# Graph propagation and a state-space block on one core: single accumulators in round two, separate banks for the block's outputs, per-row scalars computed once, row shifts on ScalarE

## The chip, the cores and the metric

The kernel runs on one core of one Trainium2 chip. The engines that matter are TensorE (PE: matmuls; PEld: its weight loads), VectorE (DVE), ScalarE (ACT), GpSimd (POOL) and the DMA queue of SyncE (SP). Each has its own queue of instructions, worked off in order; semaphores couple them. The metric is the device time of one launch in microseconds (us), lower is better.

## The reference, cut to what matters

Two layers, each added to its input. The first is two rounds of attention over a graph with 4096 nodes and 128 features; the second is a Mamba2 block (4 heads of 64, 64 states, chunks of 128 rows) over the same 4096 rows.

```python
# layer 1, on xn = layernorm(x); a, temp, h0 given; adj is 4096 x 4096 of 0 and 1
e = leaky_relu(xn @ a[:F] + (xn @ a[F:]).T, 0.2)
U = softmax(where(adj > 0, e, -9e15), axis=1)
rowsum = sum(U * 0.5 * U, axis=1)
feat = f1(U @ xn, xn, rowsum, temp)           # round one, then a soft threshold
out = f2(U @ feat, feat, rowsum, h0, temp)    # round two: a second product with U
x = x + out
# layer 2, on layernorm(x), in 32 chunks of 128 rows
z, xBC, dt = split(ln(x) @ W_in)
xh, B, C = split(silu(causal_conv4(xBC)))
Y = (C B^T * decay) (xh dt) + C h_prev * exp(cum) + xh * D   # h_prev: state carried over chunks
out = rmsnorm(Y * silu(z)) @ W_out @ W_lin + b_lin
```

The softmax is never formed. With leaky_relu the weight of an edge is one of two products, each a factor of the row times a factor of the column, so `U @ Y` is two masked matrix products: accumulator A for edges with a positive logit, accumulator C for the others. Each accumulator is scaled by a factor of its row (`roww[.., 0]`, `roww[.., 1]`) and the two are added. Y is stored as a high and a low fp32r half, so one product has 256 columns.

## The kernel before, in words

N = 4096 rows are 32 tiles of 128 (`NT`). **Start** (to about 82 us of the profile): layer norm of x, column factors `colw`, row factors `roww` (from `hcol`, made by `row_shift` on VectorE, lines 723 to 729), the products Y (`y_product` on GpSimd, `y_high` on ScalarE, line 1014, `y_low_a` on VectorE, line 626), and the first edge codes (`codes`, line 642: 128x512 codes of 1 byte from the transposed adjacency). **Round one** (to about 401 us): 8 groups of 4 tiles; adjacency comes in by DMA, ScalarE takes signs, TensorE transposes, VectorE makes codes, ScalarE and VectorE unpack them into masks A and C, and TensorE multiplies. The codes of all tiles are spilled to DRAM.

**Round two** (from about 409 us) is a software pipeline written out by hand: `schedule` calls `slot(s_, ...)` for 37 slots on every engine, 12 of them through a hardware loop body of 4 slots repeated, the others unrolled. Slot s holds the second product with U for tile s, and the stages of the Mamba2 block for the tiles s-1 to s-5. `ok[d-1]` says that the stage for tile s-d exists. In one slot TensorE runs four blocks of 8 A matmuls (line 1239) and 8 C matmuls (line 1248), with the small matmuls of the block between them. The numbered steps of one slot on TensorE are: the transpose of the normalised tile (line 1332, into bank `ps[0]`), block 0, the input projection (1341, 1343), the outputs within a chunk (1353), the state's output (1354), the state's contribution (1357, 64 output rows, into bank `ps[1]`), block 1, cumulative sums and transposes (1368 to 1372), block 2, a transpose of C (1380), block 3 with the transpose of the gated output in its middle (1389), the matrix G = C B^T (1398) and the output projection (1404, into `ps[1]` as well).

Tiles alternate between two accumulators per side, `accA[k % 2]` and `accC[k % 2]`, so block 0 of the next tile waits only for reads that are a slot old. When a tile is done, ScalarE reads A (`read_acc`, line 1044), VectorE reads C and adds (820, 837), and line 842 makes the row's result `x1` with `base` from GpSimd. GpSimd's `base_of` (lines 490 to 515) copies four numbers of the row, computes three scalars of one column each in six operations (498 to 505), and then builds `base` in six operations on 128x128 (506 to 514). After that GpSimd makes `dam` (537), `xdt`, `xdtd`, `xD`, `pstate` (545 to 551) and the output's reciprocal root (557, 558), for which VectorE's output line 833 waits. VectorE's statistics of x1 (855, 880) in turn start GpSimd's next slot (526).

VectorE's order in a slot: mask of G (813), the read of C (820), `wmix` (827), a mask, output (833), 837, 842, a mask, statistics (855), convolution steps (870) interleaved with the series for softplus and the state update (897 to 911), the gate product (962), a mask, gate and `xbc` (968, 970), a mask. A mask is line 650, 128x1024.

## Time and profile before

| | |
|---|---|
| median of 3 runs | 971.51 us (965.16 to 972.1) |
| the profiled execution, its own time | 977.07 us |
| its span in the trace | 975.1 us |
| TensorE busy, share of the span | 871.6 us, 89% |
| VectorE | 771.0 us, 79% |
| ScalarE | 595.4 us, 61% |
| GpSimd | 645.5 us, 66% |
| mean granted clock | 0.935 of 2.4 GHz |

A busy share says which engine has much to do, not which one sets the end. The chain of waits follows the execution back from its last instruction; the timeline shows for one slot who starts when, and behind whom. Positions are us from the start of the span.

### The profile page before, as it was taken

How to read it: one execution, taken by the hardware profiler on the slowest of the kernel's cores; microseconds unless marked ns; L12 is line 12 of the kernel's file. 1: busy time of each engine (PE TensorE's matmuls, PEld its weight loads, DVE VectorE, ACT ScalarE, POOL GpSimd, SP SyncE). 2: the span in 40 equal slices, each digit the busy share in tenths (PEclk: the TensorE clock that was granted, in tenths of full speed). 3: DMA queues.
4: the chain of work that ended last, by engine and by line, in shares of the span. 5: the costliest groups of instructions: out<-in, count | busy, mean ns of one | idle time of the engine just before them, and what ended most of it. 6: DMA issues, size and time to landing. Idle time of an engine off the chain costs nothing.

```text
span 975.1 us, 21990 instructions
## 1 busy us (share of the span) xinstructions
PE 871.6 (89%) x6586; PEld 776.6 (80%) x6586; DVE 771.0 (79%) x2057; ACT 595.4 (61%) x1032; POOL 645.5 (66%) x1359
## 2 busy tenths in 40 slices
PE   5858999989989999559899898999899989999976
PEld 5648999989989999549788787878778877888844
DVE  6477999979979996576989778777787778688873
ACT  3556788868778885336566556555556656565541
POOL 3550665656665667886768787877776877777743
PEclk9969999999989999859999999999989999899975
DMA  7356887968778686001111111111111111110000
GB/s 212 101 179 216 259 267 215 315 219 267 261 217 279 190 271 203 1 23 61 55 36 56 44 47 47 42 36 48 37 56 32 51 38 51 35 33 17 4 7 9
DMA packets 97386, 110.66 MB, mean 113 GB/s; under 512 B 6433, under 2 KB 89121, under 8 KB 97313
## 3 DMA queue, kind: packets, MB, share of 16 engines
q1 hardware_dynamic: 97312, 109.68, 35.6%
q8 instruction: 46, 0.75, 0.3%
q14 instruction: 28, 0.22, 0.1%
HBM read 90.79 MB, written 18.87 MB: 112 GB/s over the span
## 4 chain that ended last, share of the span: by engine, by line
POOL 44%; PE 21%; issue 15%; DVE 10%; DMA 5%; ACT 5%; POOLq 1%; DVEq 0%; ACTq 0%; SPq 0%
PE accA L1239 6%; POOL featw L510 5%; PE accC L1248 5%; DMA adj_in<-in_adj_dram 4%; POOL f_rows L547 3%; POOL adj_in L545 3%; PE ps L1186 3%; ACT edges L989 3%; POOL adj_in L549 2%; POOL featw L508 2%; POOL ywork L551 2%; POOL f_rows L558 2%; DVE code L642 2%; POOL adj_in L514 1%; POOL featw L513 1%
## 5 line engine op out<-in xcount | busy, mean ns | idle before, releaser
L1239 PE MATMUL accA<-Y,maskA 128*128 128x260 f32 (+1 forms) x2048 | 321.3, 301 | 28.6 <-DVE Y L621 18.1
L1239 PEld LDWEIGHTS accA<-Y,maskA 128*128 128x128 f32 x2048 | 273.7, 198 | 48.5 <-issue 24.6
L1025 ACT ACTIVATE maskA<-code 128x1024 fp32r<-128x1024 int8 x256 | 268.6, 1051 | 58.2 <-PE accC L1248 30.1
L1248 PE MATMUL accC<-Y,maskC 128*128 128x260 f32 (+1 forms) x2048 | 299.3, 290 | 1.4 <-DVE maskC L650 1.4
L1248 PEld LDWEIGHTS accC<-Y,maskC 128*128 128x128 f32 x2048 | 272.6, 196 | 1.9 <-DVE maskC L650 1.8
L650 DVE TENSOR_SCALAR maskC<-code 128x1024 fp32r<-128x1024 int8 x256 | 209.1, 821 | 0.3 <-issue 0.3
L642 DVE SCALAR_TENSOR_TENSOR code<-f_rows,neg_f,ps 128x512 int8<-128x512 f32 x256 | 178.4, 740 | 29.2 <-PE ps L1186 27.8
L989 ACT ACTIVATE edges<-adj_in 128x1024 bf16<-128x1024 f32 x128 | 133.3, 1045 | 27.5 <-DMA adj_in<-in_adj_dram 14.9
L1186 PE MATMUL ps<-ident,edges 128*128 128x128 bf16 x1024 | 82.7, 225 | 16.3 <-DVE code L642 10.8
L870 DVE SCALAR_TENSOR_TENSOR code<-adj_in,f_rows,code 128x128 f32<-128x128 f32 x288 | 94.9, 351 | 0.0
L1186 PEld LDWEIGHTS ps<-ident,edges 128*128 128x128 bf16 x1024 | 60.7, 101 | 27.1 <-issue 12.3
L431 POOL COPY small<-roww 128x2 f32 (+1 forms) x32 | 6.4, 199 | 86.6 <-DVE ps_sum L668 84.8
L526 POOL TENSOR_TENSOR f_rows<-f_rows,consts 128x1 f32<-128x1 f32 x32 | 8.4, 264 | 78.6 <-DVE f_rows L880 78.6
L833 DVE SCALAR_TENSOR_TENSOR adj_in<-ps,f_rows,adj_in 128x128 f32<-128x128 f32 x32 | 11.2, 351 | 62.2 <-POOL f_rows L558 62.1
L510 POOL TENSOR_TENSOR featw<-featw,adj_in 128x128 f32<-128x128 f32 x32 | 54.8, 1712 | 2.5
L1353 PE MATMUL ps<-adj_in,code 128*128 128x64 f32 x256 | 34.6, 280 | 15.2 <-issue 12.9
L1134 ACT ACTIVATE f_rows<-f_rows 128x4 f32<-128x4 f32 x32 | 6.7, 208 | 66.5 <-DVE f_rows L915 66.5
L1120 ACT COPY code<-ps 128x260 f32<-128x260 f32 x32 | 12.0, 376 | 57.3 <-PE ps L1343 57.3
L1353 PEld LDWEIGHTS ps<-adj_in,code 128*128 128x128 f32 x256 | 32.1, 197 | 18.1 <-issue 15.4
L537 POOL TENSOR_TENSOR f_rows<-f_rows 128x512 f32<-128x512 f32 x32 | 34.1, 1067 | 18.5 <-DVE f_rows L952 11.3
L1370 PE MATMUL ps<-f_rows 128*128 128x512 f32 x64 | 37.8, 675 | 0.0
L1357 PE MATMUL ps<-f_rows,code 128*64 128x256 f32 x64 | 24.1, 464 | 15.1 <-DVE adj_in L833 15.1
(199 smaller groups left out, 1588.5 us busy)
## 6 DMA issues: line engine op xcount, KB each, us to landing
adj_in<-in_adj_dram SPq DMA_DIRECT2D x128, 512.0 KB, 4.5
edge_codes<-code SPq DMA_DIRECT2D x8, 2048.0 KB, 10.0
code<-edge_codes SPq DMA_DIRECT2D x32, 512.0 KB, 3.3
xn<-in_x_dram SPq DMA_DIRECT2D x4, 512.0 KB, 5.6
adj_in<-in_x_dram SPq DMA_DIRECT2D x32, 64.0 KB, 1.8
adj_in<-in_L_gnn_h_dram SPq DMA_DIRECT2D x32, 64.0 KB, 1.9
out_dram<-adj_in SPq DMA_DIRECT2D x32, 64.0 KB, 1.6
f_rows<-in_L_ffn_W_in_dram SPq DMA_DIRECT2D x1, 192.0 KB, 6.5
```

The costliest lines, as they stand in the source:

```text
L510: link(g.tensor_tensor(featw[:, 0], featw[:, 0], x_in[:, k % 2], ALU.add))
L537: g.tensor_tensor(dam, upto.unsqueeze(1).broadcast_to([P, NH, P]), tiny[:, 2 + k % 2, NH:2 * NH].unsqueeze(2).broadcast_to([P, NH, P]), AL ...
L642: v.scalar_tensor_tensor(out=code[:, par, :, jt * P:(jt + 1) * P], in0=f1_rows[:, rows].rearrange("p (i r) -> p i r", i=IT), scalar=neg_f2 ...
L650: v.tensor_scalar(maskC[:, b % MASKS], src, 2.0, None, ALU.is_equal).then_inc(S["maskC_ready"], 1)
L870: ins = v.scalar_tensor_tensor(out=conv[:, cb], in0=hist[:, k2, cb, tap:tap + P], scalar=conv_wt[:, cb, tap:tap + 1], in1=conv[:, cb], op0 ...
L989: s.activation(edges[:, h % 4], adj_in[:, h % 4], ACT.Sign).then_inc(S["signed"], 1)
L1025: s.activation(maskA[:, b % MASKS], src, ACT.Relu, bias=-2.0).then_inc(S["maskA_ready"], 1)
L1186: m = t_.matmul(ps[jt % TRB][:, it * P:(it + 1) * P], edges[:, b % 4, it, j * P:(j + 1) * P], ident2[:], start=True, stop=True)
L1239: t_.matmul(accA[k][:, 0:2 * cols], maskA[:, b % MASKS, l * P:(l + 1) * P], Y[:, jt, 0, :, 0:cols], start=jt == 0, stop=jt == NT - 1)
L1248: m = t_.matmul(accC[k][:, 0:2 * cols], maskC[:, b % MASKS, l * P:(l + 1) * P], Y[:, jt, 1, :, 0:cols], start=jt == 0, stop=jt == NT - 1)
L1353: t_.matmul(ps[0][:, h * HD:(h + 1) * HD], wmix[:, h], xdt[:, h * HD:(h + 1) * HD], start=True, stop=True)
L1370: t_.matmul(ps[3][:, 0:NH * P], after, dam.rearrange("p h w -> p (h w)"), start=True, stop=True)
```

## The change

In round two every tile uses `accA[0]` and `accC[0]`; the second pair is given to the block: the state's contribution and the transpose of the normalised tile go to `accA[1]`, the output projection to `accC[1]`. Block 0 now waits until ScalarE has read A and VectorE has read C of the tile just finished; a new semaphore `a_done` lets ScalarE read A before the C matmuls of block 3 are over, and `c_read` tells of VectorE's read. C is no longer transposed by TensorE and copied by ScalarE: VectorE makes a second, zero-padded `cT` directly from the convolution's output (64x128, one more instruction), and the matmuls with it have the full 128 rows. GpSimd computes the per-row scalars for all 32 rows at once before round two (six operations on 128x32). The row shifts move from four VectorE instructions to two ScalarE ones, and ScalarE makes the first high halves of Y earlier.

```diff
+            r_all, zn_all, rho_all, kap_all = (row_out[:, :, i] for i in range(4))
+            link(g.tensor_tensor(kap_all, rho_all, over_rows(1, 2), ALU.mult))
+            link(g.tensor_tensor(kap_all, kap_all, over_rows(8, 9), ALU.add))
+            link(g.tensor_tensor(rho_all, kap_all, over_rows(10, 11), ALU.mult))
+            link(g.tensor_tensor(rho_all, rho_all, over_rows(1, 2), ALU.add))
+            link(g.tensor_tensor(r_all, r_all, rho_all, ALU.mult))
+            link(g.tensor_tensor(zn_all, r_all, zn_all, ALU.mult))
...
-            g.memset(state[0:DS, 0], 0.0)
+            g.memset(state[:], 0.0)
+            g.memset(cT, 0.0)
...
-                link(g.tensor_copy(small[:, 8:12], row_out[:, bass.ds(row, 1), :].rearrange("p a b -> p (a b)")))
-                r, zn, rho = (small[:, i:i + 1] for i in (8, 9, 10))
-
-                link(g.tensor_tensor(kap, coef[:, 1:2], rho, ALU.mult))
-                link(g.tensor_tensor(kap, kap, coef[:, 8:9], ALU.add))
-                link(g.tensor_tensor(wz, kap, coef[:, 10:11], ALU.mult))
-                link(g.tensor_tensor(wz, wz, coef[:, 1:2], ALU.add))
-
-                wait(pool, "x1_done", s_ - 1)
-                link(g.tensor_tensor(w, wz, r, ALU.mult))
-                link(g.tensor_tensor(wz, w, zn, ALU.mult))
...
-            def row_shift():
-
-                step(v.tensor_scalar(hcol[:, 0], fcol[:, :, 0], grow[:, 6:7], 1.0 - SLOPE, ALU.add, ALU.mult))
-                link(v.tensor_scalar(hcol[:, 1], fcol[:, :, 0], grow[:, 6:7], SLOPE - 1.0, ALU.add, ALU.mult))
-                v.tensor_scalar(hcol[:, 0], hcol[:, 0], 0.0, -SHIFT, ALU.min, ALU.add)
-                v.tensor_scalar(hcol[:, 1], hcol[:, 1], 0.0, None, ALU.min).then_inc(S["roww_done"], 1)
-                end_chain()
...
-                if ok[4]:
-                    dve.wait_ge(S["p_o"], s_ - 4)
                 if ok[3]:
 
                     dve.wait_ge(S["p_g"], s_ - 3)
...
                     dve.wait_ge(S["base_done"], T + 1)
-                    halves = step(v.scalar_tensor_tensor(
-                        out=part, in0=accC[kt][:, 0:2 * F].rearrange("p (a b) -> p a b", a=2),
-                        scalar=roww[:, bass.ds(row, 1), 1:2].rearrange("p a b -> p (a b)"), in1=acc_s[:, kt, :, 0:F], op0=ALU.mult, op1=ALU.add))
+                    dve.wait_ge(S["mm_done"], T * NB + (R1 + NB))
+                    v.scalar_tensor_tensor(
+                        out=part, in0=accC[0][:, 0:2 * F].rearrange("p (a b) -> p a b", a=2),
+                        scalar=roww[:, bass.ds(row, 1), 1:2].rearrange("p a b -> p (a b)"), in1=acc_s[:, kt, :, 0:F],
+                        op0=ALU.mult, op1=ALU.add).then_inc(S["c_read"], 1)
...
+                    wait(dve, "p_y", s_ - 3)
+                    v.scalar_tensor_tensor(out=cT[0:DS, k2], in0=gate_t[DS:P, CB - 1], scalar=1.0, in1=conv[DS:P, CB - 1], op0=ALU.add,
+                                           op1=ALU.mult).then_inc(S["conv_ready"], 1)
...
+                if q == 0:
+
+                    s.activation(hcol[:, 0], fcol[:, :, 0], ACT.Relu, bias=grow[:, 8:9], scale=SLOPE - 1.0)
+                    s.activation(hcol[:, 1], fcol[:, :, 0], ACT.Relu, bias=grow[:, 9:10], scale=1.0 - SLOPE).then_inc(S["roww_done"], 1)
...
-
-                    act.wait_ge(S["p_ct"], s_ - 2)
-                    s.copy(cT[0:DS], ps[1][0:DS, 2 * P:3 * P]).then_inc(S["cT_ready"], 1)
...
-                            wait(pe, "acc_read", s_ + (NT - 1))
-                            if isinstance(s_, int) and s_ < 2:
-                                pe.wait_ge(S["summed"], s_ + (NT - 1))
-                            wait(pe, "x1_done", s_ - 1)
+                            if isinstance(s_, int) and s_ == 0:
+                                pe.wait_ge(S["acc_read"], NT - 1)
+                                pe.wait_ge(S["summed"], NT - 1)
+                            else:
+                                pe.wait_ge(S["acc_read"], s_ + NT)
+                                pe.wait_ge(S["c_read"], s_)
...
-                    t_.matmul(ps[0][:, DI:2 * DI], cT[0:DS], state[0:DS, c], start=True, stop=True)
-                    if ok[4]:
-                        pe.wait_ge(S["out_done"], s_ - 4)
-                    t_.matmul(ps[1][0:DS, 0:DI], xl[:, DI:DI + DS], xdtd, start=True, stop=True).then_inc(S["p_y"], 1)
+                    t_.matmul(ps[0][:, DI:2 * DI], cT[:, c], state[:, c], start=True, stop=True)
+                    t_.matmul(accA[1][:, 0:DI], xl[:, DI:DI + P], xdtd, start=True, stop=True).then_inc(S["p_y"], 1)
...
-                    t_.matmul(ps[1][0:DS, 2 * P:3 * P], xl[:, DI + DS:DI + 2 * DS], ident[:], start=True, stop=True).then_inc(S["p_ct"], 1)
...
-                    t_.matmul(ps[1][:, 0:P], xbc[0:DS, (k - 3) % 2, CB - 1, :], cT[0:DS], start=True, stop=True).then_inc(S["p_g"], 1)
+                    pe.wait_ge(S["conv_ready"], s_ - 2)
+                    t_.matmul(ps[1][:, 0:P], xbc[:, (k - 3) % 2, CB - 1, :], cT[:, (k - 3) % 2], start=True, stop=True).then_inc(S["p_g"], 1)
```

Three places of the instruction order, before and then of the change. First TensorE at the head of a slot, from the waits ahead of block 0 (lines 1231 and 1238; `Y,maskA` and `Y,maskC` are the block) to the state's contribution (1357, now 1369). In the change the wait for `acc_read` stands one row ahead of those shown.

```order
L1231 ISA [waits x1_done,acc_read]
L1239 MATMUL accA<-Y,maskA 128x256 [waits maskA_ready]
L1239 MATMUL accA<-Y,maskA 128x256 x7
L1248 MATMUL accC<-Y,maskC 128x256 [waits maskC_ready]
L1248 MATMUL accC<-Y,maskC 128x256 x7
L1338 REGISTER_ALU [waits xT_ready]
L1341 MATMUL ps<-f_rows,adj_in 128x260 [waits yT_ready,exp_done]
L1343 MATMUL ps<-adj_in,f_rows 128x128 x3
L1353 MATMUL ps<-adj_in,code 128x64 [waits cT_ready,st_done,xdt_ready,mix_ready]
L1353 MATMUL ps<-adj_in,code 128x64 x3
L1354 MATMUL ps<-code,adj_in 128x256
L1357 MATMUL ps<-f_rows,code 64x256 [waits out_done]
```

```order
L1238 ISA [waits c_read]
L1246 MATMUL accA<-Y,maskA 128x256 [waits maskA_ready]
L1246 MATMUL accA<-Y,maskA 128x256 x7
L1257 MATMUL accC<-Y,maskC 128x256 [waits maskC_ready]
L1257 MATMUL accC<-Y,maskC 128x256 x7
L1352 REGISTER_ALU [waits xT_ready]
L1355 MATMUL ps<-f_rows,adj_in 128x260 [waits yT_ready,exp_done]
L1357 MATMUL ps<-adj_in,f_rows 128x128 x3
L1367 MATMUL ps<-adj_in,code 128x64 [waits st_done,y_read,xdt_ready,mix_ready]
L1367 MATMUL ps<-adj_in,code 128x64 x3
L1368 MATMUL ps<-code,f_rows 128x256
L1369 MATMUL accA<-f_rows,code 128x256
```

The wait for the output (`out_done`) has left the state's contribution, and block 0 has got a wait for `c_read`. Next VectorE at the turn from one slot to the next: the mask of G, the read of accumulator C, `wmix`, a mask and the output (line 833, now 832).

```order
L813 TENSOR_TENSOR adj_in<-ps,f_rows 128x128 [waits p_g,p_o]
L818 REGISTER_ALU
L819 REGISTER_ALU [waits acc_read]
L820 ISA [waits base_done]
L820 SCALAR_TENSOR_TENSOR ywork<-accC,roww,acc_s 128x256
L827 TENSOR_TENSOR code<-code,adj_in 128x512 [waits p_y,exp_done,vch]
L762 ISA
L224 REGISTER_ALU [waits codes_in1]
L650 TENSOR_SCALAR maskC<-code 128x1024 [waits mm_done]
L224 REGISTER_ALU [waits rs_ready]
L833 SCALAR_TENSOR_TENSOR adj_in<-ps,f_rows,adj_in 128x128 [waits stored0]
```

```order
L809 TENSOR_TENSOR adj_in<-ps,f_rows 128x128 [waits p_g]
L814 REGISTER_ALU
L815 REGISTER_ALU [waits acc_read]
L816 REGISTER_ALU [waits base_done]
L817 ISA [waits mm_done]
L817 SCALAR_TENSOR_TENSOR ywork<-accC,roww,acc_s 128x256
L825 TENSOR_TENSOR code<-code,adj_in 128x512 [waits p_y,exp_done,vch]
L760 ISA
L224 REGISTER_ALU [waits codes_in1]
L659 TENSOR_SCALAR maskC<-code 128x1024 [waits mm_done]
L224 REGISTER_ALU [waits rs_ready,p_o]
L832 SCALAR_TENSOR_TENSOR adj_in<-accC,f_rows,adj_in 128x128 [waits stored0]
```

The read of C keeps its place, now with a wait for the C matmuls; the wait for the output projection has moved behind it. Last ScalarE in the start: copies of the row logits (`f_rows`), signs (`edges`), high halves of Y.

```order
L993 COPY f_rows<-accC 128x512 [waits f1_done]
L989 ACTIVATE edges<-adj_in 128x1024 [waits tr_done,adj_in0]
L993 COPY f_rows<-accA 128x512 [waits f1_done]
L993 COPY f_rows<-accC 128x512 [waits f1_done]
L989 ACTIVATE edges<-adj_in 128x1024 [waits tr_done,adj_in1]
L993 COPY f_rows<-accA 128x512 [waits f1_done]
L993 COPY f_rows<-accC 128x512 [waits f1_done]
L993 COPY f_rows<-accA 128x512 [waits f1_done]
L1014 CAST Y<-ywork 128x8x128 [waits yA_prod]
L1014 CAST Y<-ywork 128x8x128 [waits yC_prod]
```

```order
L995 COPY f_rows<-accC 128x512 [waits f1_done]
L1015 CAST Y<-ywork 128x8x128 [waits yA_prod]
L991 ACTIVATE edges<-adj_in 128x1024 [waits tr_done,adj_in0]
L995 COPY f_rows<-accA 128x512 [waits f1_done]
L1015 CAST Y<-ywork 128x8x128 [waits yC_prod]
L995 COPY f_rows<-accC 128x512 [waits f1_done]
L991 ACTIVATE edges<-adj_in 128x1024 [waits tr_done,adj_in1]
L995 COPY f_rows<-accA 128x512 [waits f1_done]
L995 COPY f_rows<-accC 128x512 [waits f1_done]
L995 COPY f_rows<-accA 128x512 [waits f1_done]
L1075 ACTIVATE hcol<-fcol,grow 128x32
L1076 ACTIVATE hcol<-fcol,grow 128x32
```

The first high half of Y stands ahead of the first sign instead of behind all copies, and the two row shifts stand behind the copies.

## Rows read from the trace of the kernel before

**Rows 1.** The chain that ended last, shares of the span by engine (POOLq: its queue).

```profile
POOL 44%; PE 21%; issue 15%; DVE 10%; DMA 5%; ACT 5%; POOLq 1%; DVEq 0%; ACTq 0%; SPq 0%
```

**Rows 2.** Busy time by stretch: one early slot; then 24 slots of the steady pipeline.

```profile
495.80:510.50 14.70, 14.65 (x107) 12.64 (x106) 12.74 (x41) 8.81 (x21) 10.93 (x22) 1.00 0.16 50
525.90:918.00 392.10, 366.52 (x2498) 314.23 (x2497) 306.18 (x1033) 228.21 (x529) 297.05 (x553) 0.97 0.13 40
```

**Rows 3.** Timeline of GpSimd, one slot: start, us, engine, line, operation [idle before <- releaser].

```profile
606.09 0.20 POOL L526 TENSOR_TENSOR f_rows<-f_rows,consts 128x1 f32<-128x1 f32 x1 [2.54 <-DVE f_rows L880]
607.32 0.25 POOL L495 COPY small<-row_out 128x4 f32 x1
609.58 0.40 POOL L506 TENSOR_TENSOR featw<-xn,small 128x128 f32<-128x128 f32 x1 [0.18 <-POOL small L505]
611.33 2.60 POOL L510 TENSOR_TENSOR featw<-featw,adj_in 128x128 f32<-128x128 f32 x1
615.20 1.05 POOL L537 TENSOR_TENSOR f_rows<-f_rows 128x512 f32<-128x512 f32 x1 [0.25 <-POOL adj_in L514]
622.59 0.28 POOL L526 TENSOR_TENSOR f_rows<-f_rows,consts 128x1 f32<-128x1 f32 x1 [2.38 <-DVE f_rows L880]
```

**Rows 4.** Timeline of VectorE in the same slot.

```profile
611.53 0.67 DVE L650 TENSOR_SCALAR maskC<-code 128x1024 fp32r<-128x1024 int8 x1
614.21 0.29 DVE L813 TENSOR_TENSOR adj_in<-ps,f_rows 128x128 f32<-128x128 f32 x1 [0.59 <-PE ps L1404]
615.17 0.48 DVE L820 SCALAR_TENSOR_TENSOR ywork<-accC,roww,acc_s 128x256 f32<-128x256 f32 x1 [0.67 <-POOLq L515]
620.35 0.35 DVE L833 SCALAR_TENSOR_TENSOR adj_in<-ps,f_rows,adj_in 128x128 f32<-128x128 f32 x1 [2.53 <-POOL f_rows L558]
622.07 0.35 DVE L870 SCALAR_TENSOR_TENSOR code<-adj_in,f_rows,code 128x128 f32<-128x128 f32 x1
```

**Rows 5.** Timeline of TensorE in the early slot of rows 2, in which it is never idle.

```profile
500.84 0.38 PE L1389 MATMUL ps<-ident,f_rows 128*128 128x128 f32 x2
503.10 1.20 PE L1239 MATMUL accA<-Y,maskA 128*128 128x256 f32 x8
505.53 0.83 PE L1343 MATMUL ps<-adj_in,f_rows 128*128 128x128 f32 x6
507.13 0.70 PE L1354 MATMUL ps<-code,adj_in 64*128 64x256 f32 x2
```

**Rows 6.** Timeline of ScalarE in the slot of rows 3.

```profile
612.20 0.38 ACT L1164 COPY adj_in<-ps 128x256 f32<-128x256 f32 x1 [1.11 <-PE ps L1389]
613.82 0.47 ACT L1044 ACTIVATE acc_s<-accA,roww 128x256 f32<-128x256 f32 x1
617.34 0.38 ACT L1120 COPY code<-ps 128x260 f32<-128x260 f32 x1 [1.79 <-PE ps L1343]
619.19 0.20 ACT L1131 COPY adj_in<-adj_in 128x9 f32<-128x9 f32 x1
```

**Rows 7.** Timeline of VectorE in the early slot of rows 5: the same last part of a slot.

```profile
499.74 0.94 DVE L650 TENSOR_SCALAR maskC<-code 128x1024 fp32r<-128x1024 int8 x1
501.88 1.53 DVE L650 TENSOR_SCALAR maskC<-code 128x1024 fp32r<-128x1024 int8 x1
503.33 0.28 DVE L813 TENSOR_TENSOR adj_in<-ps,f_rows 128x128 f32<-128x128 f32 x1
```

**Rows 8.** Groups by shape over the 24 slots of rows 2: busy us, mean ns.

```profile
L510 POOL TENSOR_TENSOR featw<-featw,adj_in 128x128 f32<-128x128 f32 x24 | 50.4, 2101 | 1.9
```

**Rows 9.** Timeline of VectorE in the start.

```profile
44.38 1.23 DVE L626 TENSOR_TENSOR Y<-ywork,Y 128x1024 fp32r<-128x1024 f32 x1 [3.17 <-ACT Y L1014]
48.30 1.87 DVE L725 TENSOR_SCALAR hcol<-fcol,grow 128x32 f32<-128x32 f32 x1
54.24 0.17 DVE L728 TENSOR_SCALAR hcol<-hcol 128x32 f32<-128x32 f32 x1
```

**Rows 10.** The chain of waits near the end of the kernel: start, us, what.

```profile
962.73 0.73 PE ps L1404 x4
```

More of the change, by code:

```diff
@@ L182, in gnn_ffn_kernel @@
         ztan = y_space.take(DI)
-        cT = adj_space.take(P)
+        cT = rows_space.take(2, P)
         gate = rows_space.take(2, DI)
@@ L365, in link, with step_to @@
                 pool.wait_ge(S["pch"], chain[0])
+            def step_to(ins):
+                chain[0] += 1
+                ins.then_inc(S["pch"], 1)
             def end_chain():
@@ L841, in slot @@
                     wait(dve, "x1b_done", T - 1)
-                    v.scalar_tensor_tensor(out=x1[:, kt], in0=part[:, 0], scalar=small[:, 14 + kt:15 + kt], in1=base[:, kt],
+                    v.scalar_tensor_tensor(out=x1[:, kt], in0=part[:, 0], scalar=row_out[:, bass.ds(row, 1), 0:1].rearrange("p a b -> p (a b)"), in1=base[:, kt],
                                            op0=ALU.mult, op1=ALU.add).then_inc(S["x1_done"], 1)
@@ L1009, in _, with y_high_one @@
             s.copy(Y[:, :, :, 0, F:XC], colw[:].rearrange("p s t c -> p t s c")).then_inc(S["ycol_hi"], 1)
-            def y_high(q):
-                for side in range(2):
-                    act.wait_ge(S["yC_prod" if side else "yA_prod"], q + 1)
-                    s.copy(Y[:, q * JB:(q + 1) * JB, side, 0, 0:F], y_first(q, side)).then_inc(S["yC_hi" if side else "yA_hi"], 1)
+            def y_high_one(q, side):
+                act.wait_ge(S["yC_prod" if side else "yA_prod"], q + 1)
+                s.copy(Y[:, q * JB:(q + 1) * JB, side, 0, 0:F], y_first(q, side)).then_inc(S["yC_hi" if side else "yA_hi"], 1)
             def y2_high(q, prods):
@@ L1238, in products @@
                     jt = ch * JB + l
-                    t_.matmul(accA[k][:, 0:2 * cols], maskA[:, b % MASKS, l * P:(l + 1) * P], Y[:, jt, 0, :, 0:cols],
-                              start=jt == 0, stop=jt == NT - 1)
+                    m = t_.matmul(accA[k][:, 0:2 * cols], maskA[:, b % MASKS, l * P:(l + 1) * P], Y[:, jt, 0, :, 0:cols],
+                                  start=jt == 0, stop=jt == NT - 1)
+                if cols == F and ch == NB - 1:
+                    m.then_inc(S["a_done"], 1)
                 if between is not None:
@@ L1329, in slot @@
                     pe.wait_ge(S["xn2_ready"], s_ - 1)
+                    if isinstance(s_, int) and s_ == 2:
+                        pe.wait_ge(S["acc_read"], NT)
+                        pe.wait_ge(S["summed"], NT)
                     if ok[4]:
-                        pe.wait_ge(S["y_read"], s_ - 4)
-                    t_.transpose(ps[0][:, 0:P], xn2[:, c], ident[:]).then_inc(S["p_xT"], 1)
+                        pe.wait_ge(S["st_done"], s_ - 4)
+                    t_.transpose(accA[1][:, DI:DI + P], xn2[:, c], ident[:]).then_inc(S["p_xT"], 1)
                 block(0)
```

64 lines of the change are left out of this document (33 added, 31 removed).

## The prediction

> **What bounds the kernel now.** I read the chain of waits first. GpSimd has 44% of it, TensorE 21% [rows 1], although GpSimd is busy for only 66% of the span. So in round two it is not work but a ring of waits that sets the pace. The busy times by stretch put a size to it: 24 steady slots take 392.1 us, 16.34 each, while the early slot took 14.70 with TensorE busy for 14.65 of it [rows 2]. TensorE could thus run 1.6 us a slot faster; something else holds it.
>
> The timelines of one slot show what. GpSimd starts with line 526 at 606.09 and again at 622.59, 16.50 later, each time behind VectorE's statistics (880) [rows 3]. It works without a real gap from 606.09 until VectorE's output (833), which waits 2.53 us for it and starts at 620.35; 1.7 us later VectorE is at the convolution (870, 622.07), and with it the statistics that start GpSimd again [rows 4]. The ring is GpSimd 14.3 us, VectorE 2.2 us. Every operation in it costs its full time.
>
> **The change, part by part.**
>
> *Scalars for all rows.* The copy (495) starts at 607.32 and line 506 at 609.58 [rows 3]: 2.26 us a slot leave the ring. The six operations on 128x32 and two larger memsets are paid once, bounded by 0.25 us each (a 128x4 copy) and 1.05 each (the 128x512 product): 2 to 8 us. They stand where the first slot's own small operations, 2.3 us or more, go. I book 0 for the entry to round two.
>
> *The output leaves the path of the state's contribution.* TensorE no longer stands at line 1357 until VectorE's output is made, the last step behind GpSimd. With the 2.26 us gone, GpSimd's line 537 would start early enough to meet its other wait, VectorE's dt, made just before the mask at 611.53. So GpSimd from 611.4, 5.0 us of work as now (615.20 to 620.2), is done at 616.4, 3.8 us before the present time. GpSimd's ring falls to 12.7 us and stops deciding. What is late next is the question.
>
> *TensorE's own work.* It loses the transpose of C: two matmuls of the shape of 1389, 0.38 us [rows 5]. The state's output on 64 rows takes 0.70 us for two matmuls of 256 columns [rows 5]; eight of 256 columns on 128 rows take 1.20, so two could take 0.3. The state's contribution on 64 columns and G are of the same kind. The worst is no gain, the best 0.4 for each of the three; I take 0.1 in all beside the transpose: 14.65 becomes about 14.15.
>
> *The single accumulators add a stop.* Now block 0 starts 1.88 us after the transposes of the gated output (500.84 + 0.38 to 503.10) [rows 5]. ScalarE starts behind them at 612.20 and has read A at 613.82 + 0.47 = 614.29, 2.1 us later [rows 6]. VectorE reads C after that, 0.48 us [rows 4]. So block 0 can start 2.7 us behind the transposes: a stop of 0.85 us. TensorE's slot is 14.15 + 0.85 = 15.0, less where savings behind the transposes only lengthen the stop; 14.8 to 15.0.
>
> *A new ring.* Since block 0 now waits for VectorE's read, this ring closes: block 0 starts, the projection is done 3.26 us later (503.10 to 505.53 + 0.83) [rows 5]; ScalarE, which waits for it, has read it and made the halo 2.1 us after that (617.34 to 619.39) [rows 6]; VectorE goes from the first convolution step to the mask behind the gate product in 5.96 us (622.07 less one slot of 16.50, to 611.53) [rows 3, 4]. Then two masks, gate, `xbc` and the new `cT` lead to the mask of G and the read of C. From 611.53 to the end of the last mask is 2.1 us in that slot, since the next instruction stood ready and idle for 0.59 before 614.21 [rows 4]; in the early slot it was 3.6 (499.74 to 503.33) [rows 7]. `cT` adds 0.3 (a third of a 128x384 one would be less, a 128x128 one 0.35 [rows 4]). With 0.2 for the mask of G, 0.4 for the read and 0.2 for semaphores: 3.26 + 2.1 + 5.96 + 2.1 + 0.3 + 0.8 = 14.5 with the short end, 16.0 with the long one, to which a slower `cT` adds up to 0.3.
>
> Which end? In the first slot GpSimd's line 510 took 2.60 us beside VectorE's masks: GpSimd stood and VectorE ran free. In the early slot a mask took 1.53 us instead of 0.67 [rows 7]: VectorE stood. Line 510's mean over the 24 slots is 2.10 us [rows 8]; between 2.6 and about 0.6 that is GpSimd standing in three slots of four. After the change GpSimd's lines 537 to 547 run beside the same masks. So I weight 3 to 1: 0.75 x 14.9 (TensorE's figure, which is above the ring's 14.5) + 0.25 x 16.2 = 15.2.
>
> By the Trainium skill, Advanced Engine Details and Errata, section VectorE Performance Modes, GpSimd and VectorE block each other where a VectorE instruction uses its second SBUF port. Taken as a rule that VectorE always pays, it makes this slot 16.2 and the gain vanish; the trace has both outcomes, so this stands as a rival.
>
> *The steady pipeline:* 24 x (16.34 - 15.2) = 27 us less.
>
> *The start.* VectorE waits 3.17 us for the first high half of Y, then makes the four row shifts from 48.30 to 54.24, 1.9 to 2.3 us each for three of them and 0.17 for the last [rows 9]: beside GpSimd's large products three tiny operations cost 6 us. All 9 us leave VectorE. ScalarE takes over: two operations of about 0.2, but its copies, casts and signs then come close behind each other, so I count 5 us of the 9, and 3 to 7 as the range. Round one behind it is bound by TensorE and keeps the gain.
>
> *The drain.* VectorE's mask of G no longer waits for the output projection: 0.73 us at full or half clock a slot [rows 10] on the last chains. With the transpose gone, 3 us (1 to 5). ScalarE's copy of C goes as well; ScalarE is busy for 61% of the span and this place waits for TensorE, so I cost it at nothing. The row loads on SyncE's queue wait for `base_done`, which comes earlier; they are two of 64 KB a slot and stay hidden.
>
> **Sum.** 27 + 5 + 3 = 35 us. The profiled execution took 977.07 us (span 975.1 and 2.0 around it), so 942; the median of the runs is 971.51, 5.6 below it, and the same difference gives **937 us**.
>
> **The rivals.**
>
> *VectorE runs free all the time* (14.8 a slot): 37 + 5 + 3 = 45, 927 us. For it: line 510's mean. Against it: the early slots.
>
> *VectorE always pays for the shared port* (16.2 a slot): the new ring takes back what GpSimd's gives. 24 x 0.14 + 8 = 11, 960 us. For it: the mask of 1.53 us, and that now three operations of 1 us of GpSimd lie there instead of one.
>
> *The clock.* The granted clock was 0.97 over the steady slots [rows 2], that is TensorE was at the lower of its two levels for about 6% of them, after stops. Now a stop comes in every slot and TensorE is in the ring. If one slot in two has 3.4 us at half speed, of which TensorE's projection feels 1.5, that is 12 x 1.5 = 18: 955 us. The Trainium skill (TensorE: Matmul & The Clock Gate, A second HAM failure mode) describes short idling between groups of matmuls as enough for this; no run here has yet shown it with a stop as short as 0.85 us, and the early slots held 1.00.
>
> *Slower than before.* The new ring goes through VectorE once, and VectorE pays not only at the masks but also in its nine convolution steps, beside which GpSimd's operations on 128x128 now fall (they fell beside the state update). The four instructions at the slot's end lost 1.5 us together [rows 4, 7], 0.4 each; five steps at 0.4 are 2 us more, so up to 18.2; at half of that the slot takes 17.2, 24 x 0.86 - 8 = +13: 984 us. It decides as soon as the ring is above 16.7 us.
>
> **Chances.** Forecast (15.0 to 15.8 a slot) 0.46; VectorE free 0.20; always paying 0.18; the clock 0.08; slower 0.08. About 1%, 9.7 us, is what a measurement of this kernel can tell from no change. Faster by more than that: the forecast, the free case, the clock and nearly half of the paying case, 0.81. Within: 0.12. Slower by over 1%: 0.07. The range leaves out a tenth on each side: from below the free case with the larger start (7) and drain (5), 918, to above the paying case with the smaller ones, 965. The forecast's own range is 926 to 950.
>
> **What the profile after would show.** Right: no wait of TensorE in front of the state's contribution; VectorE waits at the output for GpSimd for little or nothing; a stop of about 0.9 us before block 0, behind VectorE's read; GpSimd's share of the chain far below 44%, VectorE's and TensorE's far above; the first 16 codes done some 5 us earlier. A stop before block 0 of 2 us or more, behind VectorE, and masks above 1 us mean that the shared port pays. Wrong altogether: slots still 16.5 us apart with line 526 behind line 558, which would say that GpSimd's ring was not cut.

## The result, and the profile after

The changed kernel takes 1080.74 us, median of 4 runs (1080.34 to 1081.64), against 968.92 for the kernel before: a ratio of 1.115, 95% interval 1.111 to 1.120 (968.92 is the median of four runs; the 971.51 ahead was that of three of them). The forecast was 937 us; the kernel is slower by 112 us instead of faster by 35.

Where the time went is read from one instruction that comes once in each slot of round two, VectorE's aggregation of the statistics. Its first and last time before, and after (start, us, engine, line):

```profile
443.59 0.18 DVE L880 BATCH_NORM_AGGREGATE f_rows<-f_rows 128x2 f32<-128x6 f32 x1
...
930.75 0.17 DVE L880 BATCH_NORM_AGGREGATE f_rows<-f_rows 128x2 f32<-128x6 f32 x1
```

```profile
436.08 0.18 DVE L879 BATCH_NORM_AGGREGATE f_rows<-f_rows 128x2 f32<-128x6 f32 x1
...
1035.63 0.17 DVE L879 BATCH_NORM_AGGREGATE f_rows<-f_rows 128x2 f32<-128x6 f32 x1
```

Up to the first one 7.5 us are gained. What follows the last is 43.0 us of the span of 1078.6, and was 44.4 of 975.1: 1.4 gained. The 31 slots between take 599.6 us instead of 487.2: 112.4 lost. All of the loss lies there. The 24 slots that the prediction counts (392.1 us before) take 480.9, so 89 us are theirs; the six slots ahead of them, which it left at no change, lose 24, and the last one gains 0.5.

The chain of waits after, by engine, answers to [rows 1]:

```profile
PE 31%; DVE 29%; issue 14%; POOL 11%; ACT 10%; DMA 3%; DVEq 1%; POOLq 0%; ACTq 0%; SPq 0%
```

GpSimd's share fell from 44% to 11%, and the long pieces of it that are left lie ahead of the steady slots, the last one at 415 us. Its ring was cut, as forecast. Busy time from 500 to 850 us, the changed kernel (length, then TensorE, its weight loads, VectorE, ScalarE, GpSimd; granted clock third from the end):

```profile
500.00:850.00 350.00, 281.05 (x1811) 259.12 (x1811) 265.12 (x779) 161.12 (x374) 164.72 (x283) 0.86 0.11 37
```

No engine is near full, and the clock is 0.86, where it was 0.97 [rows 2]. One slot, 20.40 us from one start of block 0 to the next. TensorE:

```profile
611.41 0.27 PE L1346 MATMUL accA<-ident,adj_in 128*128 128x128 f32 x1
614.92 2.07 PE L1246 MATMUL accA<-Y,maskA 128*128 128x256 f32 x8 [3.23 <-DVE ywork L817]
616.79 1.91 PE L1257 MATMUL accC<-Y,maskC 128*128 128x256 f32 x8
619.36 1.49 PE L1357 MATMUL ps<-adj_in,f_rows 128*128 128x128 f32 x6
626.01 1.20 PE L1246 MATMUL accA<-Y,maskA 128*128 128x256 f32 x8
629.91 0.44 PE L1394 MATMUL ps<-ident,f_rows 128*128 128x128 f32 x2 [0.78 <-DVE f_rows L961]
635.32 2.07 PE L1246 MATMUL accA<-Y,maskA 128*128 128x256 f32 x8 [3.23 <-DVE ywork L817]
```

Block 0 waits 3.23 us for VectorE's read of C (817), and then its eight matmuls take 2.07 us instead of the 1.20 that the same eight take at 626.01: behind the stop TensorE is at 1.2 GHz (the granted clock from 614.92 to 617 is 0.50 of full speed). So it is in most slots, though not in all: behind the same stop of 3.24 us, block 0 at 695.01 and at 834.98 takes 1.30 us, and these slots are some 19 us long. ScalarE, VectorE and GpSimd in the same slot:

```profile
620.88 0.38 ACT L1130 COPY code<-ps 128x260 f32<-128x260 f32 x1 [7.69 <-PE ps L1357]
```

```profile
622.81 0.34 DVE L869 SCALAR_TENSOR_TENSOR code<-adj_in,f_rows,code 128x128 f32<-128x128 f32 x1
625.04 0.56 DVE L869 SCALAR_TENSOR_TENSOR code<-adj_in,f_rows,code 128x128 f32<-128x128 f32 x1
629.77 1.53 DVE L659 TENSOR_SCALAR maskC<-code 128x1024 fp32r<-128x1024 int8 x1
631.23 0.83 DVE L967 SCALAR_TENSOR_TENSOR f_rows<-ywork,code 128x256 f32<-128x256 f32 x1
631.98 0.96 DVE L969 SCALAR_TENSOR_TENSOR code<-code 128x384 f32<-128x384 f32 x1
632.96 0.61 DVE L971 SCALAR_TENSOR_TENSOR f_rows<-code 64x128 f32<-64x128 f32 x1
633.60 0.99 DVE L659 TENSOR_SCALAR maskC<-code 128x1024 fp32r<-128x1024 int8 x1
634.52 0.28 DVE L809 TENSOR_TENSOR adj_in<-ps,f_rows 128x128 f32<-128x128 f32 x1
634.72 0.47 DVE L817 SCALAR_TENSOR_TENSOR ywork<-accC,roww,acc_s 128x256 f32<-128x256 f32 x1
```

```profile
623.33 0.28 POOL L533 TENSOR_TENSOR f_rows<-f_rows,consts 128x1 f32<-128x1 f32 x1 [8.46 <-DVE f_rows L879]
629.55 1.21 POOL L544 TENSOR_TENSOR f_rows<-f_rows 128x512 f32<-128x512 f32 x1 [1.88 <-DVE f_rows L951]
630.72 1.06 POOL L552 TENSOR_TENSOR adj_in<-code,f_rows 128x256 f32<-128x256 f32 x1
```

These are the steps of the new ring of the prediction, in its order, and they add up to the whole slot: block 0 to the end of the projection 5.93 us (614.92 to 619.36 + 1.49), ScalarE to the first convolution step 1.96, convolution to mask 6.96, mask to mask of G 4.75 (629.77 to 634.52), mask of G and read 0.80. Together 20.40. GpSimd starts line 544 at 629.55, 0.22 us ahead of VectorE's mask. In 27 slots in a row it is 0.14 to 0.23 us ahead, and in all of them the mask takes 1.53 or 1.54 us.

### The profile page after: what moved, and what is told of

The parts are those of the page before. It is cut to its first block, busy times and chain, and to the rows that moved or that the text cites. A ratio compares the mean times of both kernels' runs of the same rounds, so it can differ in the third digit from the quotient of the medians.

```text
span 1078.6 us, 21604 instructions
## 1 busy us (share of the span) xinstructions
PE 883.9 (82%) x6522; PEld 820.8 (76%) x6522; DVE 833.2 (77%) x2087; ACT 582.7 (54%) x1002; POOL 561.6 (52%) x1142
## 4 chain that ended last, share of the span: by engine, by line
PE 31%; DVE 29%; issue 14%; POOL 11%; ACT 10%; DMA 3%; DVEq 1%; POOLq 0%; ACTq 0%; SPq 0%
PE accA L1246 10%; PE accC L1257 9%; DVE code L869 9%; PE ps L1357 3%; ACT code L1135 3%; DMA adj_in<-in_adj_dram 3%; DVE f_rows L948 3%; PE ps L1355 2%; PE ps L1193 2%; ACT edges L991 2%; DVE maskC L659 2%; ACT maskA L1026 2%; DVE f_rows L941 2%; ACT adj_in L1132 1%; DVE code L651 1%
## 5 line engine op out<-in xcount | busy, mean ns | idle before, releaser
L1246 PE MATMUL accA<-Y,maskA 128*128 128x260 f32 (+1 forms) x2048 | 335.7, 310 | 130.2 <-DVE ywork L817 64.8
L1246 PEld LDWEIGHTS accA<-Y,maskA 128*128 128x128 f32 x2048 | 288.9, 206 | 140.4 <-issue 112.9
L1257 PE MATMUL accC<-Y,maskC 128*128 128x260 f32 (+1 forms) x2048 | 315.8, 301 | 1.1 <-DVE maskC L659 1.1
L1257 PEld LDWEIGHTS accC<-Y,maskC 128*128 128x128 f32 x2048 | 289.4, 208 | 1.3 <-DVE maskC L659 1.3
L659 DVE TENSOR_SCALAR maskC<-code 128x1024 fp32r<-128x1024 int8 x256 | 220.5, 865 | 3.5 <-PE accC L1257 2.5
L869 DVE SCALAR_TENSOR_TENSOR code<-adj_in,f_rows,code 128x128 f32<-128x128 f32 x288 | 114.6, 419 | 0.0
L1171 ACT COPY adj_in<-ps 128x256 f32<-128x256 f32 x32 | 12.0, 374 | 71.8 <-PE ps L1394 71.8
L1357 PEld LDWEIGHTS ps<-adj_in,f_rows 128*128 128x128 f32 x192 | 42.7, 296 | 5.2
L1394 PE MATMUL ps<-ident,f_rows 128*128 128x128 f32 x64 | 14.7, 313 | 32.7 <-DVE f_rows L961 31.5
L1357 PE MATMUL ps<-adj_in,f_rows 128*128 128x128 f32 x192 | 41.1, 376 | 0.0
```

Source lines behind the costliest of these rows:

```text
L659: v.tensor_scalar(maskC[:, b % MASKS], src, 2.0, None, ALU.is_equal).then_inc(S["maskC_ready"], 1)
L869: ins = v.scalar_tensor_tensor(out=conv[:, cb], in0=hist[:, k2, cb, tap:tap + P], scalar=conv_wt[:, cb, tap:tap + 1], in1=conv[:, cb], op0 ...
L1246: m = t_.matmul(accA[k][:, 0:2 * cols], maskA[:, b % MASKS, l * P:(l + 1) * P], Y[:, jt, 0, :, 0:cols], start=jt == 0, stop=jt == NT - 1)
L1257: m = t_.matmul(accC[k][:, 0:2 * cols], maskC[:, b % MASKS, l * P:(l + 1) * P], Y[:, jt, 1, :, 0:cols], start=jt == 0, stop=jt == NT - 1)
L1357: m = t_.matmul(ps[3][:, cb * P:(cb + 1) * P], w_xbc[:, cb * P:(cb + 1) * P], xn2T, start=True, stop=True)
```

## The experiments

Kernels are compared with runs of the kernel before on the same chip (medians 969.8 to 977.4 us). A time with "3 rounds" is the median of four executions or more; any other time is that of one execution.

**Read of C earlier, products held, TensorE kept busy, the wait alone.** The changed kernel with the read moved to the end of VectorE's slot:

```diff
+                if now:
+                    dve.wait_ge(S["acc_read"], s_ + (NT + 1))
...
+                        op0=ALU.mult, op1=ALU.add).then_inc(S["c_read"], 1)
                 mask(3)
```

> The changed kernel, but VectorE reads accumulator C at the end of its own slot, behind the convolution's xbc and cT and ahead of the last mask, instead of after the mask of G in the next slot. Theory (a ring of block 0, projection, ScalarE, convolution, masks and read of C, closed by the single accumulators, sets the pace): the ring loses the last mask (0.99 us), the mask of G and the queueing behind it, about 2 us a slot, so 30 slots give 60 us: about 1020 us; if the stop of TensorE becomes short enough for its clock to stay up, up to 2.7 us a slot more, down to about 950. Rival (the pace is set by VectorE's load or by the contention with GpSimd, not by the place of the read): about 1080, unchanged.

998.89 us (3 rounds, 1.024 of before, 1.021 to 1.026): between the two times of the theory, and far from its rival. The stop fell to 2.1 us, and the clock now stays up behind most stops; behind every third or fourth it falls. Two consecutive slots of this kernel:

```profile
715.25 1.22 PE L1248 MATMUL accA<-Y,maskA 128*128 128x256 f32 x8 [2.14 <-DVE ywork L971]
...
731.86 2.07 PE L1248 MATMUL accA<-Y,maskA 128*128 128x256 f32 x8 [2.13 <-DVE ywork L971]
```

The first was followed by a slot of 16.6 us, the second by one of 18.0.

Filler matmuls in the stop of the changed kernel:

```diff
                     t_.transpose(accA[1][:, DI:DI + P], xn2[:, c], ident[:]).then_inc(S["p_xT"], 1)
+                    if ok[3] and now:
+                        pe.wait_ge(S["exp_done"], s_ - 3)
+                        for _ in range(FILL):
+                            t_.matmul(ps[2][:, :]..., ident2[:], edges[:, 0, :, 0:P], start=True, stop=True)
```

> The changed kernel with 12 matmuls of 512 columns added in each slot, whose results nobody reads, in front of block 0, where TensorE stands for 3.2 us. They take 2.6 us at the full clock, so that TensorE is busy in its stop. Theory (the stop in every slot puts the clock to its lower level, and block 0 and the projection take 5.93 instead of 3.26 us): the granted clock of round two rises from 0.86 towards 1, and up to 2.7 us a slot come back, 80 us in all: about 1000 us. Rival (the clock's fall is a by-product and the ring is long for VectorE's sake): 1080 us or a little more.

1015.9 us. TensorE does 77 us more work (28 slots of 2.75 us) and the kernel is 65 us faster. The fillers, and block 0 behind them:

```profile
703.96 2.75 PE L1351 MATMUL ps<-edges,ident 128*128 128x512 bf16 x12
707.37 1.22 PE L1247 MATMUL accA<-Y,maskA 128*128 128x256 f32 x8 [0.65 <-DVE ywork L818]
```

The granted clock is 1.00 from 500 to 850 us and the slot 17.7 us. So the lower clock is 2.7 of the changed kernel's 20.4, and the ring without it is 17.7.

GpSimd's products held back until VectorE has made xbc and cT:

```diff
                     wait(pool, "dt_ready", s_ - 1)
+                    wait(pool, "conv_ready", s_ - 1)
```

> The changed kernel, but GpSimd starts its decay and state products (lines 544 to 558) only when VectorE has finished the convolution of the row, so that they don't run beside VectorE's mask, gate, xbc and cT. Theory (contention for the shared port makes that stretch 4.75 us instead of 2.4 to 3.9): the masks fall from 1.53 and 0.99 to 0.7, the slot loses 1 to 2 us, 30 to 60 us in all: 1020 to 1050 us. Rival 1 (no contention there): masks as long as now, 1080. Rival 2 (GpSimd's products come too late for TensorE's state output): above 1080.

980.6 us, a larger gain than expected: the slot is 16.3 us, the stop 1.36, and the clock 1.00. VectorE and GpSimd:

```profile
715.71 0.69 DVE L660 TENSOR_SCALAR maskC<-code 128x1024 fp32r<-128x1024 int8 x1
716.32 0.42 DVE L968 SCALAR_TENSOR_TENSOR f_rows<-ywork,code 128x256 f32<-128x256 f32 x1
716.65 0.55 DVE L970 SCALAR_TENSOR_TENSOR code<-code 128x384 f32<-128x384 f32 x1
717.21 0.29 DVE L972 SCALAR_TENSOR_TENSOR f_rows<-code 64x128 f32<-64x128 f32 x1
717.53 0.69 DVE L660 TENSOR_SCALAR maskC<-code 128x1024 fp32r<-128x1024 int8 x1
```

```profile
717.64 1.49 POOL L545 TENSOR_TENSOR f_rows<-f_rows 128x512 f32<-128x512 f32 x1 [3.98 <-DVE f_rows L972]
```

The stretch that took 4.75 us takes 2.43 (715.71 to 718.14). Here the second mask starts 0.11 us ahead of GpSimd's product, keeps its 0.69, and the product takes 1.49; in the changed kernel, where the product starts first, it takes 1.21 and the mask 1.53.

The kernel before with the wait alone:

```diff
-                            wait(pe, "acc_read", s_ + (NT - 1))
-                            wait(pe, "x1_done", s_ - 1)
+                            pe.wait_ge(S["acc_read"], s_ + NT)
+                            wait(pe, "c_read", s_)
```

> The kernel before, with both pairs of accumulators, its old banks, its scalars per row and its transpose of C, and one thing of the change alone: block 0 of round two waits until ScalarE and VectorE have read the accumulators of the row just before (it waited for the row two before). Theory (the closed ring is the whole loss): slots of 19 us or more, 1060 us or more, with TensorE's granted clock below 0.90 in round two. Rival (the loss comes from the other parts: the banks, the zero-padded C on 128 rows, cT on VectorE, the order of the output): 971 to 1000 us.

987.5 us. My theory that the closed ring is the whole loss fell. The slots are still 16.6 us: GpSimd's old ring brings its products only after the masks, and the new ring fits into the old slot. Beside the masks lies line 510, as in the kernel before; in 18 slots it is the one to stand (2.6 us, the masks 0.68), in nine the mask takes 0.95 instead.

**Where GpSimd is early and the ring open.** Of the change only the scalars for all rows and the start:

```diff
+            link(g.tensor_tensor(kap_all, rho_all, over_rows(1, 2), ALU.mult))
...
-                link(g.tensor_copy(small[:, 8:12], row_out[:, bass.ds(row, 1), :]...))
...
-            def row_shift():
```

> The kernel before with two parts of the change and no more: the base scalars of all rows at once, and the row shifts on ScalarE with its order at the start. Both pairs of accumulators, the old banks and the transpose of C stay. Theory (the closed ring is what turns GpSimd's earlier work into a loss, since VectorE's longer instructions reach block 0 only through it): the slot falls below 16.5 us, by at most the 2.3 us that leave GpSimd, less what VectorE now pays beside it: 940 to 955 us. Rival (GpSimd's products beside VectorE's masks cost as much whatever TensorE waits for): 965 to 980 us.

931.91 us (3 rounds, 0.955 of before, 0.948 to 0.962): the fastest kernel of the study. VectorE pays just as in the changed kernel:

```profile
716.12 1.54 DVE L658 TENSOR_SCALAR maskC<-code 128x1024 fp32r<-128x1024 int8 x1
717.58 0.84 DVE L965 SCALAR_TENSOR_TENSOR f_rows<-ywork,code 128x256 f32<-128x256 f32 x1
```

```profile
500.00:850.00 350.00, 344.27 (x2445) 297.64 (x2446) 341.39 (x1022) 222.73 (x517) 232.67 (x378) 1.00 0.15 47
```

but the slot is 14.9 us: block 0 does not wait for it, TensorE and VectorE are both busy for 98% of the stretch. The kernel before can take GpSimd's gain; the changed one can't.

On this kernel, the ring closed on both reads, and on A's read alone:

```diff
-                            wait(pe, "acc_read", s_ + (NT - 1))
+                            pe.wait_ge(S["acc_read"], s_ + NT)
-                            wait(pe, "x1_done", s_ - 1)
+                            wait(pe, "c_read", s_)
```

> The kernel with the scalars and the start alone (931.9 us, slots of 14.9), and one thing more: block 0 waits until ScalarE and VectorE have read the accumulators of the row just before. Theory (neither the wait alone, 987.5, nor GpSimd's earlier work alone, 931.9, makes the loss, but both together: the products beside VectorE's masks lengthen a ring that now goes through block 0): slots of 19 to 20.5 us, 1060 to 1085 us in all, granted clock below 0.90. Rival (the loss comes from banks, padding or the order of the output, which this kernel does not have): 932 to 990 us.

1006.28 us, slots of 17.1: 74 us more than the open ring, but 74 less than the changed kernel. It lies between the two expectations, so neither hit. The stop is 2.1 us, and the clock is 1.00 from 500 to 850 us:

```profile
718.00 1.22 PE L1244 MATMUL accA<-Y,maskA 128*128 128x256 f32 x8 [2.12 <-DVE ywork L817]
```

> The kernel with the scalars and the start alone, and block 0 waits for ScalarE's read of accumulator A of the row just before, but not for VectorE's read of C. Theory (only VectorE's read, which stands behind masks, gate, xbc and the mask of G, closes the long ring; ScalarE has read A some 0.3 us after block 0 starts now): 930 to 945 us. Rival (any wait for the row just before makes the stop that lowers the clock): above 1000 us.

939.75 us, slots of 15.1: as the theory said. Waiting for A's read costs 0.2 us a slot, waiting for C's the rest.

C made directly by VectorE, added to the open kernel and to the closed one:

```diff
-                    v.scalar_tensor_tensor(out=xbc[:, k2], ...).then_inc(S["conv_ready"], 1)
+                    v.scalar_tensor_tensor(out=xbc[:, k2], ...)
+                    v.scalar_tensor_tensor(out=cT[0:DS, k2], in0=gate_t[DS:P, CB - 1], scalar=1.0, in1=conv[DS:P, CB - 1], ...)
...
-                    t_.matmul(ps[1][0:DS, 2 * P:3 * P], xl[:, DI + DS:DI + 2 * DS], ident[:], ...)
```

> The kernel with the scalars and the start alone, and of the change also C made directly by VectorE, zero-padded, on 128 rows, without TensorE's transpose and ScalarE's copy; both pairs of accumulators stay. Theory (VectorE has hardly an idle moment in a slot of 14.9 us and sets it; TensorE only waits 0.3 to 0.4 us for it): cT adds 0.6 us of VectorE, so 940 to 950 us. Rival (TensorE sets the slot, and loses two matmuls of 0.4 us and a wait of 0.4): 908 to 920 us.

940.66 us (3 rounds, 0.964 of before, 0.959 to 0.969), 8.7 us more than without it. TensorE's busy time in the same stretch falls by 31 us, VectorE's stays at 98%:

```profile
500.00:850.00 350.00, 312.94 (x2339) 287.88 (x2338) 343.86 (x1007) 208.95 (x483) 215.81 (x368) 1.00 0.15 46
```

VectorE sets the slot there, and what TensorE loses is no gain.

> The kernel with the scalars and the start alone, block 0 closed on both reads as before (1006.3 us, slots of 17.1, granted clock 1.00, a stop of 2.1 us), and C made directly by VectorE as in the change. Theory (these four are all that counts: cT is 0.6 us longer in the ring, the stop grows to about 2.7 us or more and TensorE's clock falls in block 0): slots of 19 to 20.4 us, 1055 to 1085 us. Rival 1 (the clock stays up): 17.7 us a slot, 1022 to 1028 us; then the rest of the changed kernel's loss lies in its banks, its padding or its order of the output.

1083.87 us, slots of 20.4, clock 0.86 from 500 to 850 us. This kernel has both pairs of accumulators and the old banks, and it is as slow as the changed one, with the same stop of 3.24 us (in this slot the clock falls within block 0; in most the block takes 2.07 us):

```profile
716.68 1.32 PE L1245 MATMUL accA<-Y,maskA 128*128 128x256 f32 x8 [3.24 <-DVE ywork L818]
717.80 1.92 PE L1254 MATMUL accC<-Y,maskC 128*128 128x256 f32 x8
```

The banks, the padding of the state's contribution and the order of the output therefore have no share in the loss that can be seen. From the other side, cT taken out of the ring of the changed kernel:

```diff
+                if ok[2]:
+                    v.scalar_tensor_tensor(out=cT[0:DS, 1 - k2], ...).then_inc(S["conv_ready"], 1)
                 if ok[3]:
                     dve.wait_ge(S["vch"], masked)
```

> The changed kernel, but VectorE makes cT behind its read of C in the next slot instead of ahead of the last mask. Theory: 0.6 us leave the ring, the stop before block 0 shrinks from 3.24 to about 2.1 to 2.6 us, at which the clock stayed up or fell in one slot of three: 17.1 to 18 us a slot, 1000 to 1035 us. Rival (the clock falls after any stop of 2 us): 19.8 us a slot, 1060 us.

1008.49 us, slots of 17.1, clock 0.99. One instruction of 0.61 us, in another place, is worth 72 us. The stop here is

```profile
705.61 1.23 PE L1247 MATMUL accA<-Y,maskA 128*128 128x256 f32 x8 [2.61 <-DVE ywork L817]
```

and block 0 runs at the full clock.

**Further orders of GpSimd.** The read earlier and the products held, together:

> The changed kernel with VectorE's early read of C and GpSimd's products held until cT, but the base where it was. Theory: the stop of 1.36 us before block 0, which was left with the products held alone, goes; the ring xbc, products, output, convolution (16.2 us) stays: 975 to 980 us. Rival (the ring through the projection was the one that decided with the products held): 940 to 960 us.

979.8 us, as the theory said, and the chain runs through the second ring (GpSimd's products and the convolution steps). But its stop did not go: it is still 1.28 us, since VectorE's read of C now waits 1.18 us for ScalarE's read of A. GpSimd's base behind its products (`base_of` moved to the slot's end) missed each time:

> The changed kernel with three shifts of order: VectorE reads C at the end of its slot; GpSimd's decay and state products wait for xbc and cT; and GpSimd makes the base of the row behind those products, so that it doesn't run beside VectorE's convolution. Theory (contention where it lies in the ring): the masks and gate stay at 1.8 us instead of 3.9, the late convolution steps go from 0.56 to 0.35 us, the stop before block 0 goes, and the slot falls from 16.3 (with the products held alone) to 15.5, where GpSimd's own wait for xbc and VectorE's for its output take over: 950 to 960 us. Rival (the hold itself is the pace: xbc, products, output, convolution): 975 to 980, as with the products held alone.

1034.96 us (3 rounds, 1.063 of before, 1.055 to 1.071). The convolution did run free (steps of 0.34 us), but VectorE's wait for the base stood ahead of the state mix, which I had not looked at, and VectorE stands there 4.2 us a slot (the waits: total, times, longest):

```profile
DVE code L820 <- POOLq L522: 122.9, 29, 6.1
```

> As the kernel with the read, the held products and the base behind them, and one more: VectorE makes the output behind the convolution steps instead of ahead of the sum for x1, so that it no longer waits there for GpSimd's power. Theory (the ring xbc, products, output, convolution is the next to decide): slot 14.9 to 15.2 us, 935 to 950 us in all. Rival (TensorE or the ring through the projection is already the bound): the same time as the kernel without this step, to within 3 us.

1034.85 us (3 rounds, 1.062 of before), the same for the same reason (123.2 us at line 820), so the output's place was not tested. Without the early read the same wait stands in the ring of block 0:

> The changed kernel with the products held and the base behind them, but the read of C left where the change has it. Theory: VectorE's convolution runs free, 0.6 us a slot less than with the products held alone (980.6): 960 to 965 us. Rival (the hold itself is the pace): 978 to 982 us.

1198.23 us. With the wait moved to where the base is used, on the kernel with scalars and start:

> The kernel with the scalars and the start alone, but GpSimd makes the base behind its products instead of ahead of them, and VectorE waits for it only where it adds it to x1. Theory (VectorE sets the slot, and its late convolution steps take 0.55 us beside GpSimd's base and 0.34 alone): 0.7 us a slot less, 905 to 920 us. Rival (the contention moves to the operations that now run beside the base): 928 to 935 us.

964.6 us (3 rounds, 0.987 of before, 0.982 to 0.992), 33 more than without the move. VectorE still waits 2.2 us a slot for a base that is made too late:

```profile
DVE adj_in L839 <- POOLq L521: 66.5, 30, 2.5
```

**The start alone:**

> The kernel before with the part at the start alone: row shifts on ScalarE, and its order of the high halves. Theory: 5 us less, 3 to 7, since round one behind it is bound by TensorE and keeps the gain. Rival (the gain is lost in round one, whose later chunks wait for ScalarE): 0 to 1 us less.

962.9 us (3 rounds, ten executions) against 969.84, ratio 0.993 (0.991 to 0.996), 4 to 9 us less, with 7 in the middle, at the upper end of what was expected. The codes that started at 54.33 start at

```profile
47.66 5.36 DVE L644 SCALAR_TENSOR_TENSOR code<-f_rows,neg_f,ps 128x512 int8<-128x512 f32 x8 [2.70 <-PE ps L1184]
```

Not all of this can be put down to the change. In the kernel with the wait alone, whose start is that of the kernel before, the same codes start at 51.49, so this place moves by 2.8 us between executions without the change, against 6.7 here. And the profiled spans differ by 11.7 us: 3.1 less ahead of the first aggregation, 1.7 more behind the last, and 10.2 less in the 31 slots between, where GpSimd's line 510 stands for 2.6 us in nine slots instead of 18. Those slots are 16.5 us long, most of the others 15.5. What decides that number no run shows.

## Why the prediction was wrong, point by point

*What bounds the kernel now* was right. GpSimd's ring set the pace, and cutting it takes a slot from 16.3 to 14.9 us where nothing takes its place (931.91 us).

*The start* came out in its range, 5 forecast, 4 to 9 measured, but the traces don't show that all of it comes from there. *The drain* gave 1.4 instead of 3.

*The new ring* was found, with the right steps in the right order, and mis-sized: 14.5 to 16.0 us forecast, 17.7 measured at full clock and 20.4 with the clock's fall. The step that failed is "Which end?":

- Masks, gate, xbc and cT: between 2.4 and 3.9 us forecast, 4.75 measured beside GpSimd's products and 2.43 with them held. I took the mean duration of line 510 [rows 8] for a chance, 3 to 1, that VectorE runs free. That mean belongs to one instruction in the order of the kernel before: there it took 2.6 us in 18 of the 24 slots and 0.6 in six. In the changed kernel another instruction, line 544, meets the mask. It is released by dt 0.22 us before the mask starts, and VectorE pays at five instructions in a row, in every one of 27 slots.
- The convolution: 5.96 us forecast, 6.96 measured, since GpSimd's base now lies beside it (0.56 us for a step of 0.34). I had put this into the rival alone.
- Together the ring at full clock is 17.7 us, inside the range of the rival that ends slower (17.2 to 18.2, chance 0.08). Its mechanism was right, but 984 us was too low even for its own part (1015.9 with the clock held up), because it reckoned with 17.2 us, and for 24 slots alone: with the clock up the six slots ahead of them lose 20 us too. And it left out the clock.

Who starts first in the trace does not decide who pays. In the kernel before, line 510 too starts 0.20 us ahead of the mask, in both outcomes. In one slot it took 2.60 us and the mask 0.67 (611.33 and 611.53 [rows 3, 4]); in the early slot the mask at 499.74 took 0.94 [rows 7], and line 510 ahead of it

```profile
499.54 0.59 POOL L510 TENSOR_TENSOR featw<-featw,adj_in 128x128 f32<-128x128 f32 x1
```

So the mix of the old order said nothing of the new one, and the order of the starts would not have told it either. What picks the outcome stays open.

*The clock* was a rival of its own, priced for one slot in two at 1.5 us, on top of a stop of 0.85. It depends on the ring: the stop is what the ring is longer than TensorE's work. With the ring at 17.7 the stop is some 3 us, the clock falls in most slots, block 0 and the projection are in the ring, and take 5.93 instead of 3.26 us; 2.7 us in most slots. The two rivals were one chain of causes, and I priced them apart.

*The single accumulators* as such cost little: the wait for A 0.2 us a slot (939.75). It is C, read behind everything VectorE does late in its slot, that ties block 0 to those instructions.

From the kernel with scalars and start, the loss adds up in runs: ring open 931.91 us, closed on both reads 1006.28, with cT in the ring 1083.87. In the changed kernel fillers take back the clock's part (1015.9). The ring alone on the kernel before costs 987.5. The changed kernel is thus slower for an interaction of three of its parts: GpSimd's earlier start puts its products beside VectorE's late instructions, the single C makes TensorE wait for those, and cT adds the 0.6 us at which the clock goes. Any one of them taken back gives most of the loss back: products held 980.6, cT elsewhere 1008.49, both accumulators doubled 940.66 (with the start, the scalars and cT).

By the Trainium skill, Advanced Engine Details and Errata, section GPSIMD Details, GpSimd conflicts with VectorE instructions in a two-port mode or with two SBUF inputs. The traces agree: convolution steps and gate, with two such inputs, slow down (0.34 to 0.56, 0.42 to 0.83 us), while the read of C, whose one input comes from PSUM, takes 0.47 to 0.48 in all of them. The mask, with one SBUF input, slows down as well (0.69 to 1.53 us); whether it runs in a two-port mode no run shows.

What stays open, besides which of the two engines waits: which stops lower the clock. In the changed kernel itself stops of the same 3.24 us lower it in most slots and not in all. Stops of 2.6 us left it up in nearly all slots of one kernel, stops of 2.1 let it fall in about every third slot of another, whose slots are shorter; the runs don't settle the rule.

## What to carry to other kernels

Before you shorten one engine's ring, write down which instructions of the others its work will then lie beside, and count what each of two neighbours pays, slot by slot: a mean duration over the old order is no chance for the new one. Where the outcome can't be told, reckon with the case in which every instruction of the ring pays. Halving a buffer that is read at the end of a long sequence ties the producer to the whole sequence; ask of each reader how late it comes, since here waiting for one (A) cost 8 us and for the other (C) 67 more. Where a stop of TensorE comes out of such a sum, count the work behind it at half clock too, and try the parts of a change singly: here two of them alone make the kernel 4.5% faster than before.

## What the runs showed of the hardware that was not expected

- Beside each other one of the two engines pays nearly all of it. A 128x1024 mask takes 0.69 us when it starts 0.11 us before GpSimd's 128x512 product (which then takes 1.49), and 1.53 when it starts 0.22 us behind it (which then takes 1.21). But the order of the starts in the trace is no rule: 0.20 us behind GpSimd's 128x128 line 510, the same mask takes 0.68 in 18 slots of the kernel before (line 510 then 2.6) and 0.95 in eight (line 510 then 0.6).
- The clock's answer to stops is a cliff: with one instruction of 0.61 us more in the ring, and stops of 3.24 instead of 2.61 us, the slot grows from 17.1 to 20.4 us. TensorE can also be given work to stay at 2.4 GHz: twelve unused matmuls, 2.75 us a slot, made the kernel 65 us faster.
